# An adaLN transformer block in split fp32r: the head of the program rearranged

## The reference, cut to what matters

```
mod = (silu(c) @ wmod).reshape(B, 6, 1, -1)        # sa, ca, ga, sb, cb, gb; ga and gb are kept at |g| >= 0.25
h = layernorm(x) * (1 + ca) + sa
q, k, v = split(h @ c_attn_w + c_attn_b)
# a first softmax over the first 128 channels of q and k gives cam_ctx; tanh(cam_ctx * gate)
# is added to q, so to the scores of the second softmax over all 256 channels
x = x + ga * (softmax(scores) @ v @ c_proj_w + c_proj_b)
h = layernorm(x) * (1 + cb) + sb
x = x + gb * (gelu(h @ proj1.T + b1) @ proj2.T + b2)
```

## Time and profile before

| what | value |
|---|---|
| median of 3 runs | 324.19 us (323.69 to 325.05) |
| time of the profiled execution | 323.65 us |
| its span, first to last instruction | 321.9 us |
| PE busy over the span | 310.5 us (96%) |
| DVE busy | 216.4 us (67%) |
| ACT busy | 155.2 us (48%) |
| POOL busy | 103.5 us (32%) |
| granted PE clock, mean over the span | 0.999 |

### The profile page before, as it was taken

One profiled execution on the slowest core, in us unless ns is written; L12 is line 12 of the kernel. 1 busy time (PEld: TensorE's weight loads), 2 busy tenths in 40 slices (PEclk: granted clock), 3 DMA queues, 4 the chain that ended last, 5 costly groups with the idle time before them and its releaser, 6 DMA issues.

```text
span 321.9 us, 5165 instructions
## 1 busy us (share of the span) xinstructions
PE 310.5 (96%) x2004; PEld 282.0 (88%) x2004; DVE 216.4 (67%) x425; ACT 155.2 (48%) x259; POOL 103.5 (32%) x117
## 2 busy tenths in 40 slices
PE   2899999999999999999999999999999999999996
PEld 2688988888999998898899988898999899899895
DVE  4986688996555668895753789888664576753531
ACT  2444565564324327915931486555532244860930
POOL 2401656144445656236011032140021232603311
PEclk9999999999999999999999999999999999999999
DMA  7910020420000000010001000000000000001001
GB/s 235 372 47 2 0 65 3 193 70 0 2 0 2 1 2 1 0 35 33 2 16 49 1 3 2 0 0 2 0 2 0 2 0 2 0 1 52 16 6 61
DMA packets 7992, 10.30 MB, mean 32 GB/s; under 512 B 672, under 2 KB 6560, under 8 KB 7968
## 3 DMA queue, kind: packets, MB, share of 16 engines
q1 hardware_dynamic: 7968, 9.97, 9.2%
HBM read 7.35 MB, written 2.10 MB: 29 GB/s over the span
## 4 chain that ended last, share of the span: by engine, by line
PE 84%; DVE 10%; ACT 2%; issue 1%; DMA 1%; SPq 0%; DVEq 0%
PE a_ps L187 13%; PE a_ps L186 13%; PE a_ps L185 13%; PE s_ps L185 11%; PE s_ps L187 11%; PE s_ps L186 11%; PE t_ps L880 7%; DVE nmax L632 2%; PE t_ps L823 2%; PE t_ps L783 2%; DMA wmod_raw<-wmod 1%; DVE ht_lo L593 1%; DVE k_lo L602 1%; DVE th L614 1%; DVE modc L671 1%
## 5 line engine op out<-in xcount | busy, mean ns | idle before, releaser
L447 ACT ACTIVATE pt_hi<-t_ps 128x512 fp32r<-128x512 f32 x64 | 34.9, 596 | 67.7 <-PE t_ps L880 67.6
L632 DVE TENSOR_REDUCE nmax<-s_ps 128x1 f32<-128x1024 f32 x32 | 39.0, 1219 | 15.2 <-PE s_ps L187 15.1
L626 DVE TENSOR_TENSOR pt_lo<-t_ps,pt_hi 128x512 fp32r<-128x512 f32 x64 | 40.9, 680 | 1.3 <-ACT pt_hi L447 1.3
L457 ACT ACTIVATE prob<-s_ps,nmax 128x1024 f32<-128x1024 f32 x32 | 35.8, 1118 | 11.7 <-DVE nmax L632 11.5
L311 POOL TENSOR_SCALAR prob<-prob,rinv 128x1024 f32<-128x1024 f32 x16 | 18.0, 1125 | 64.7 <-DVE rinv L636 64.7
L185 PE MATMUL s_ps<-k_hi,q_hi 128*128 128x512 f32 x96 | 38.3, 399 | 0.0
L187 PE MATMUL s_ps<-k_hi,q_lo 128*128 128x512 f32 x96 | 37.7, 393 | 0.0
L186 PE MATMUL s_ps<-k_lo,q_hi 128*128 128x512 f32 x96 | 37.5, 391 | 0.0
L185 PE MATMUL a_ps<-v_hi,pt_hi 128*128 128x256 f32 x128 | 36.8, 288 | 0.0
L185 PE MATMUL a_ps<-w_hi,pt_hi 128*128 128x256 f32 x128 | 36.4, 284 | 0.0
L186 PE MATMUL a_ps<-w_lo,pt_hi 128*128 128x256 f32 x128 | 36.2, 283 | 0.0
(11 more groups left out here) (118 smaller groups left out, 752.1 us busy)
## 6 DMA issues: line engine op xcount, KB each, us to landing
x_all<-x SPq DMA_DIRECT2D x4, 512.0 KB, 9.0
w_raw<-w_t SPq DMA_DIRECT2D x2, 1024.0 KB, 6.3
out<-x_all SPq DMA_DIRECT2D x16, 128.0 KB, 1.7
wmod_raw<-wmod SPq DMA_DIRECT2D x1, 1024.0 KB, 9.9
wmod_raw<-wmod SPq DMA_DIRECT2D x1, 512.0 KB, 4.5
wattn_raw<-w_attn SPq DMA_DIRECT2D x1, 512.0 KB, 6.3
...
```

Source lines behind the costliest of these rows:

```text
L447: A(pt_hi[:, (u // 2) % 2, 4 * g:4 * g + 4, (u % 2) * P:(u % 2 + 1) * P], t_bank(b, "p", 2 * u + g)[:, :].rearrange("p (t n) -> p t n", n= ...
L457: A(prob[:, u % 3, :], s_ps[u % 2][:, :], ACT.Exp, bias=nmax[:, u:u + 1], accum_out=rsum[:, u:u + 1]).then_inc(exp_ready, 1)
L626: V.tensor_tensor(pt_lo[dst], t_bank(b, "p", 2 * u + g)[:, :].rearrange("p (t n) -> p t n", n=P), f(pt_hi[dst]), ALU.subtract).then_inc(pt ...
L632: V.tensor_reduce(nmax[:, u:u + 1], s_ps[u % 2][:, :], AX.X, ALU.max, negate=True).then_inc(nmax_ready, 1)
```

## The change

The head of batch 0 is written anew, and one filler moves into it; batch 1 and everything behind unit 0 of batch 0 run the instructions that they ran before.

- **Loads.** Batch 0's x comes as four loads of two tiles. The first is issued ahead of `cols`, the second behind it; the other two stand behind `wp` in the queue.
- **Zero matmuls.** DVE fills a buffer with zeros, and PE multiplies it nine times (`warm_up(9)`) ahead of `modulation(0)`. The result is never read.
- **Norm by pairs.** Statistics, power and normed tiles are made two tiles at a time, and the first transposes follow in pairs. The small operations of the silu that DVE did are POOL's now, but for the reciprocal; so are the two broadcast copies and a part of `wv_lo`.
- **h by two engines.** `ht_hi` is written by ACT straight from PSUM with scale and shift (`h_high`), `h32` by DVE from the same bank (`h_full`), and the subtraction is DVE's as before. The same goes for blocks 0 to 3 of q and k: ACT makes both the full value and `hi`, DVE has only the subtraction (`qk_low`).
- **Products by kind.** For the q and k blocks of the first half hi·hi comes first, then the weights' `lo` part, then `fold_projection`, then `ht_lo`. `wqk_hi` and `wqk_lo` are made in two parts, the channels of blocks 0 to 3 first; POOL's second part waits for all of `xn`.
- **Four V blocks ahead.** V blocks 0 to 3 run ahead of the first scores; before there were three, and block 3 was the filler of unit 0.

The core of the diff:

```diff
-            A_JOBS += [(b, "v", t) for t in range(3)]
+            A_JOBS += [(b, "v", t) for t in range(3 if b else TH)]
...
-            if b == 0:
-                T_JOBS += [(0, "mod", 0)]
...
+            def load_x(i, t, n):
+                sp.dma_start(x_all[:, t:t + n, :], x_v[:, t:t + n, :]).then_inc(x_in[i], 16)
...
+            load_x(0, 0, 2)
             sp.dma_start(cols_sb[:, :], cols).then_inc(cols_in, 16)
-            load_x(0)
+            load_x(1, 2, 2)
             sp.dma_start(wmod1_raw[:, :, :], wm[:, :, 0:2 * E]).then_inc(wmod1_in, 16)
             sp.dma_start(wattn_raw[:, :, 0:2 * E], wa[:, :, 0:2 * E]).then_inc(wqk_in, 16)
-            load_x(1)
             sp.dma_start(wvt_raw[:, :, :], wv_t.rearrange("(c p) n -> p c n", p=P)).then_inc(wvt_in, 16)
...
+            load_x(2, 4, 2)
+            load_x(3, 6, 2)
...
+            pool.wait_ge(cols_in, 16)
+            G.tensor_scalar(lw_arg[:, :], cols_sb[:, C_W1:C_W1 + 1], DEPTH, cols_sb[:, C_W0:C_W0 + 1],
+                            ALU.mult, ALU.add).then_inc(lw_ready, 1)
+            G.tensor_scalar(bq_scaled[:, :], cols_sb[:, C_BQ:C_BQ + 2], QSCALE, 1.0, ALU.mult, ALU.mult)
+            G.tensor_tensor(gate_bias[:, :], cols_sb[:, C_BVC:C_BVC + 1], cols_sb[:, C_GATE:C_GATE + 1], ALU.mult)
+            pool.wait_ge(exps_ready, 2)
+            G.tensor_scalar(exps[:, :], exps[:, :], 1.0, 1.0, ALU.add, ALU.mult).then_inc(plus1_ready, 1)
+            pool.wait_ge(recip_ready, 1)
+            G.tensor_tensor(sct[:, :, :], cols_sb[:, C_CT:C_CT + EC * B].rearrange("p (c b) -> p c b", b=B),
+                            exps[:, 0:EC * B].rearrange("p (c b) -> p c b", b=B), ALU.mult).then_inc(sct_ready, 1)
+            G.tensor_scalar(lw_scaled[:, :], exps[:, EC * B:EC * B + 1], QSCALE, 1.0, ALU.mult, ALU.mult)
...
+            inv_std_pair(0, 0)
+            inv_std_pair(0, 1)
+            wqk_low(0)
...
+            pool.wait_ge(wv_raw_hi, 1)
+            G.tensor_tensor(wv_lo[:, :, 0:DK], wattn_raw[:, :, 2 * E:2 * E + DK], f(wv_hi[:, :, 0:DK]), ALU.subtract)\
+                .then_inc(wv_raw_lo, 1)
+            inv_std_pair(1, 0)
+            inv_std_pair(1, 1)
+            wait(pool, xn_ready, 0, 2)
+            wqk_low(1)
...
+            def h_high(r):
+                if r % 2:
+                    wait(act, ht_psum, 0, r + 1)
+                    act.wait_ge(mod_ready, 1)
+                else:
+                    wait(act, h32_ready, 0, r + 1)
+                c, n = r % 2, slice(r // 2 * HALF, (r // 2 + 1) * HALF)
+                A(ht_hi[:, c, n], t_bank(0, "h", r)[:, :], ACT.Identity,
+                  scale=modc[:, 0, c + 2:c + 3], bias=modc[:, 0, c:c + 1]).then_inc(hhi_ready, 1)
...
+            wqk_high(0)
+            h_high(1)
+            h_high(0)
+            wqk_high(1)
...
+            qk_bias(0, 0)
+            qk_high(0)
+            qk_bias(0, 1)
+            v_high(0, 0)
+            qk_high(1)
+            v_high(0, 1)
+            h_high(3)
+            h_high(2)
+            v_high(0, 2)
...
+            def h_full(r):
+                c = r % 2
+                wait(dve, ht_psum, 0, r + 1)
+                dve.wait_ge(mod_ready, 1)
+                if c:
+                    wait(dve, hhi_ready, 0, r)
+                if r >= 2:
+                    wait(dve, hlo_ready, 0, 2)
+                V.tensor_scalar(h32[:, c, :], t_bank(0, "h", r)[:, :], modc[:, 0, c + 2:c + 3], modc[:, 0, c:c + 1],
+                                ALU.mult, ALU.add).then_inc(h32_ready, 1)
+            def h_low(r):
+                wait(dve, h32_ready, 0, r // 2 * 2 + 2)
+                wait(dve, hhi_ready, 0, (2, 1, 4, 3)[r])
+                dst = (slice(None), r % 2, slice(r // 2 * HALF, (r // 2 + 1) * HALF))
+                V.tensor_tensor(ht_lo[dst], h32[:, r % 2, :], f(ht_hi[dst]), ALU.subtract).then_inc(hlo_ready, 1)
...
+            pair_stats(0, 0)
+            pair_stats(0, 1)
+            pair_norm(0, 0)
+            pair_norm(0, 1)
             mod_columns(0)
-            norm_stats(0, 1)
-            h_split(0, 0)
-            h_split(0, 1)
-            norm_apply(0, 1)
+            h_full(0)
+            h_full(1)
+            h_low(1)
+            h_low(0)
+            pair_stats(1, 0)
+            pair_stats(1, 1)
+            dve.wait_ge(wv_hi_ready, 1)
+            V.tensor_tensor(wv_lo[:, :, DK:NV], a_bank(0, "wvp", 0)[:, :].rearrange("p (c n) -> p c n", c=EC),
+                            f(wv_hi[:, :, DK:NV]), ALU.subtract).then_inc(wv_lo_ready, 1)
+            pair_norm(1, 0)
+            pair_norm(1, 1)
+            qk_low(0)
+            v_low(0, 0)
+            qk_low(1)
+            v_low(0, 1)
+            h_full(2)
+            h_full(3)
+            h_low(3)
+            h_low(2)
+            v_low(0, 2)
...
+            def warm_up(n):
+                pe.wait_ge(warm_ready, 1)
+                for _ in range(n):
+                    M(s_bank(2)[:, 0:2 * P], f32s[:, 0, 0:P], f32s[:, 0, 0:2 * P], start=True, stop=True)
...
+            def pair_transpose(g):
+                pe.wait_ge(xn_ready if g else xn_first, 1)
+                for r in range(EC):
+                    for t in range(2 * g, 2 * g + 2):
+                        last = nc.tensor.transpose(t_bank(0, "h", r)[:, t * P:(t + 1) * P],
+                                                   xn[:, t, r * P:(r + 1) * P], ident[:, :])
+                    if g:
+                        last.then_inc(ht_psum, 1)
...
+            def high_high(j, k):
+                m, h = QK_JOBS[j]
+                wait(pe, hhi_ready, 0, 2 * h + 2 - k)
+                M(s_bank(j), wqk_hi[:, k, m * P:(m + 1) * P], ht_hi[:, k, h * HALF:(h + 1) * HALF], start=k == 1, stop=False)
+            def low_high(j, k):
+                m, h = QK_JOBS[j]
+                M(s_bank(j), wqk_lo[:, k, m * P:(m + 1) * P], ht_hi[:, k, h * HALF:(h + 1) * HALF], start=False, stop=False)
+            def high_low(j, k):
+                m, h = QK_JOBS[j]
+                wait(pe, hlo_ready, 0, 2 * h + 2 - k)
+                last = M(s_bank(j), wqk_hi[:, k, m * P:(m + 1) * P], ht_lo[:, k, h * HALF:(h + 1) * HALF],
+                         start=False, stop=k == 0)
+                if k == 0:
+                    last.then_inc(qk_psum, 1)
+            def first_half():
+                pe.wait_ge(wqk_hi_ready, 1)
+                for k in (1, 0):
+                    high_high(0, k)
+                    high_high(1, k)
+                pe.wait_ge(wqk_lo_ready, 1)
+                for k in (1, 0):
+                    low_high(0, k)
+                    low_high(1, k)
+                fold_projection()
+                for k in (1, 0):
+                    high_low(0, k)
+                    high_low(1, k)
+            def second_half():
+                pe.wait_ge(mod_copied, 1)
+                for k in (1, 0):
+                    high_high(2, k)
+                for k in (1, 0):
+                    low_high(2, k)
+                for k in (1, 0):
+                    high_high(3, k)
+                for k in (1, 0):
+                    high_low(2, k)
+                for k in (1, 0):
+                    low_high(3, k)
+                for k in (1, 0):
+                    high_low(3, k)
...
+            def first_value():
+                a_free(0, "v", 0)
+                n, o = slice(0, P), a_bank(0, "v", 0)[:, 0:NV]
+                pe.wait_ge(wv_hi_ready, 1)
+                for k in range(EC):
+                    M(o, ht_hi[:, k, n], wv_hi[:, k, :], start=k == 0, stop=False)
+                    M(o, ht_lo[:, k, n], wv_hi[:, k, :], start=False, stop=False)
+                pe.wait_ge(wv_raw_lo, 1)
+                pe.wait_ge(wv_lo_ready, 1)
+                for k in range(EC):
+                    last = M(o, ht_hi[:, k, n], wv_lo[:, k, :], start=False, stop=k == EC - 1)
+                last.then_inc(v_psum, 1)
...
+            warm_up(9)
             modulation(0)
             pe.wait_ge(ident_ready, 1)
-            h_transpose(0, 0)
-            h_transpose(0, 1)
-            fold_projection()
-            pe.wait_ge(wqk_lo_ready, 1)
-            qk_project(0, 0)
+            pair_transpose(0)
+            pair_transpose(1)
+            first_half()
+            first_value()
+            v_project(0, 1)
             h_transpose(0, 2)
             h_transpose(0, 3)
+            v_project(0, 2)
             for b in range(B):
-                for j in range(1, 4):
-                    qk_project(b, j)
-                    if b == 0 and j == 1:
-                        pe.wait_ge(wv_lo_ready, 1)
-                    if j >= 1:
+                if b == 0:
+                    second_half()
+                    v_project(0, 3)```

PE at the start of the program, before. The rows name line, operation, output and inputs; `ident,xn` are the transposes and `wp_raw,wvt_raw` is `fold_projection`.

```order
L783 MATMUL t_ps<-sct,wmod_raw 128x2 x8
L823 MATMUL t_ps<-ident,xn 128x128 x8
```

(53 more changed lines are left out.)

119 lines of the change are left out of this document (64 added, 55 removed).

## The result

The changed kernel takes 322.67 us (median of 5 runs, 322.48 to 322.96) against 324.01 us of the kernel before (5 runs): a ratio of 0.996, 95% interval 0.9945 to 0.9975. That is 0.4% faster, 1.3 us where 2.4 were forecast, inside the range given, and between the forecast case and the two rivals that lose part of the gain. The profiled execution took 322.67 us, its span is 320.9 us, 1.0 less than before.

A forecast was written before the change was run, and what follows sets the result against it. PE bounds the kernel: the end is the start of its gapless stretch plus its work. First scores 1.36 us earlier plus 1.06 for V block 3 sum to 2.4: 323.65 to 321.25, on the median's scale 321.8 us; range 320.6 to 323.8.

The forecast's parts named there:

- the forecast case: Whole kernel: 321.8 us, 0.74% faster, own range 321.0 to 322.8 us; chance 0.56.
- S: Start of the first scores on PE; forecast 24.95 us, 1.36 us earlier than before.
- Loads: Head's DMA: wmod stays near 6.2 us, first x tiles near 3.6, `cols` just behind; edits cost nothing.
- Silu on POOL: Head: 8.0 + 6p us to the transposes, 9.5 with p, a small POOL operation, at 0.25; power 1.19.
- Zero matmuls: PE's head: eighteen passes from about 1.2 us, six to nine slow, end at 6.4 to 7.0 us.
- M: When DVE can begin `h_full(0)`; forecast 9.5 us, before 11.95.
- From M to D: DVE sets the stretch to D, its end of the second half's last `ht_lo`: D = M + 12.8 = 22.3.
- From D to S: Last `ht_lo` to first scores: block 2's product, drain, ACT and DVE work end last, D + 2.65 = 24.95 us.
- V block 3: Behind the first scores in unit 0: its removal there saves 1.06 us.
- The clock: Rival, PE's head: rate falls back before the products and fold; gain 0.8, 323.4 us; chance 0.13.
- POOL in DVE's way: Rival, head: addition of 1 waits out `wqk_lo`, M up to 10.7; gain 1.0, 323.2 us; chance 0.13.
- slower, since the zeros never raise the rate: Rival, head: zeros end at 8.9, M = 14.4, 326.6 us; part of the slower case, chance 0.10.

The follow-up runs named there:

- poolmove: Changed kernel with POOL's second part of the weights' low half moved behind its first division; ratio 0.9968, median 323.17 us.
- w0: Changed kernel with no zero matmuls instead of nine; ratio 1.0055, median 325.78 us.
- w7: Changed kernel with seven zero matmuls instead of nine; ratio 0.9936, median 321.77 us.
- v3filler: Changed kernel with V block 3 back as the filler of unit 0; ratio 0.9972, median 323.31 us.
- dvelate: Changed kernel with another order on DVE alone, low halves of q/k blocks 0 and 1 last; ratio 0.9921, median 321.76 us.
- bz7: Kernel before with only seven zero matmuls and their buffer added ahead of its modulation; ratio 0.9949, median 322.82 us.
- w7dvemod: Changed kernel with seven zero matmuls, the late DVE order, and POOL's weight subtraction waiting for the modulation columns; ratio 0.9936, median 321.20 us.
- bz9: Kernel before with nine zero matmuls and no other edit; ratio 0.9996, median 323.53 us.

## Why the prediction was right, and where its sum was off

**The forecast and the time.** The profiled execution was forecast at 321.25 us and took 322.67, 1.4 us more; 1.25 us of that are the first scores (26.20 for 24.95). The median is only 0.9 us above its forecast of 321.8, and that is luck: the forecast had added 0.5 us, by which the median stood above the profiled execution before, and in the changed kernel the two are equal. Of the signs named, the fold (1.89 us), the addition of 1 (0.23 us) and the first power on POOL (5.28 us) came true; the slow zero passes (12), `mod_ready` (10.32 us), the last `ht_lo`, the first scores and the span did not.

**What bounds the kernel: right.** Behind S the span is 294.7 us in the changed kernel and 294.5 to 294.7 in eight others (all with V block 3 ahead but poolmove, which has 295.0), 295.8 with the block as filler, 321.9 - 26.31 = 295.6 before. The end is S plus a constant, over six microseconds of S.

**Loads: off by 0.5.** "wmod stays near 6.2 us": it lands at 6.73 (w0), as its DMA is issued 0.57 us later; the sum had left the issue out. In the changed kernel the zeros hide it. `cols` came at 3.78 and x at 3.61 us, for which 3.6 was forecast.

**Silu on POOL: right, with a good price.** p is 0.19 to 0.27 us, the power 0.72 to 0.79; both `xn` pairs were ready by 7.94. This never came near the path, and the rival with p = 0.65 is out.

**Zero matmuls: the mis-sized term.** The step was "they end at 1.2 + 6 x 0.43 + 12 x 0.216 = 6.4 to 7.0", with six to nine of the passes at half rate. They started at 1.43, 12 of 18 passes were at half rate, the first of them 0.16 us longer than the others, and they ended at 8.0. I took that number from the fold of the kernel before, but there PE had five microseconds of other work behind it. The profiles show 7 such passes (w7, v3filler) to 12 (dvelate, the change): it differs from execution to execution, and with it M, 9.6 to 10.8 with nine zeros. M was 1.1 us late, which is nearly all that the sum is off.

**From M to D: right** (12.7 us, forecast 12.8), though `h_full` takes 0.81 and not 0.69 us. The steps between hold too: the two subtractions end at M + 3.3 (forecast 2.85), `wv_lo` at M + 6.5 (6.2), the four low halves at M + 10.0 (9.95). What `h_full` cost more, POOL cost less, 0.1 us in place of 0.3; that the sum is so close owes something to this. That DVE sets it was shown by the order on DVE. **From D to S:** 2.87 for 2.65. **V block 3:** 1.06 forecast, 1.1 shown.

**The rivals.** The clock did not fall in the profile of the changed kernel; it did in those of bz7 and w7dvemod, both with seven zeros, and, behind a wait of 2.7 us, in bz9. By the mean granted clock it fell in none of the five executions of the changed kernel. Why it holds behind nine zeros and not always behind seven is not shown. I had given this rival 0.8 us of gain left; w7dvemod, in the execution in which it fell, had 0.1 us of span left, and with the late order at that. POOL in DVE's way was priced at up to 1.4 us; where it happened in the new head it cost 0.4 us (dvelate) and 0.55 (w7), since the operation now comes in two pieces and DVE got in at their seam. "GPSIMD Engine Reference", section "Key points" of the Trainium skill, names DVE instructions in a two-port mode or with two SBUF inputs. The trace agrees for the operations from PSUM: `h_full`, which reads PSUM, took 0.81 us beside `wqk_lo` as without it. The addition of 1 has one SBUF input and was held, 2.31 us in bz9; that would be the two-port kind, and no row tells an operation's mode. The rival "slower, since the zeros never raise the rate" did not come true. It was priced at 326.6 us; w0, which has no zeros to wait for and whose rate was low until 18.6 us, took 325.78 us.
